# TensorE's expert loop: eight blocks a turn in place of two, and the next block's register values loaded among the products

## The reference

```python
gate_logits = x @ w_gate                                   # 2048 x 8
topk_vals, topk_idx = jax.lax.top_k(softmax(gate_logits), 2)
gu = jnp.einsum('bsd,edh->ebsh', x, w_gate_up)             # 256 -> 2 x 1024 for each expert
g, u = jnp.split(gu, 2, axis=-1)
act = silu(g) * u
expert_out = jnp.einsum('ebsf,efd->ebsd', act, w_down)     # 1024 -> 256
out = x + jnp.einsum('bse,ebsd->bsd', gate_probs, expert_out)
```

## Time and profile before

| | us |
|---|---|
| median of three runs | 480.5 |
| the three runs | 467.39, 480.5, 480.98 |
| the profiled execution, its own time | 467.51 |
| its span | 465.7 |
| TensorE busy, of the span | 438.6 (94%) |
| VectorE busy | 313.3 (67%) |
| ScalarE busy | 224.7 (48%) |
| GpSimd busy | 191.2 (41%) |

### The profile page before, as it was taken

The page is one execution under the profiler, slowest core; times in us unless marked ns, Lnnn a source line. Parts: engine busy times, 40 slices in busy tenths (PEclk is TensorE's granted clock), DMA queues, the critical chain, the costliest instruction groups (busy, mean ns, idle before and its releaser), DMA issues.

```text
span 465.7 us, 10519 instructions
## 1 busy us (share of the span) xinstructions
PE 438.6 (94%) x2336; PEld 357.0 (77%) x2337; DVE 313.3 (67%) x813; ACT 224.7 (48%) x484; POOL 191.2 (41%) x210
## 2 busy tenths in 40 slices
PE   8899788899999999999999999999999999999980
PEld 4688444688888888888888888888888888888870
DVE  2678998887587568857775467867775487745530
ACT  2577863564554345536543345636543364434330
POOL 4355203445553445433453335533453435543211
PEclk9999679899999999999999999999999999999996
DMA  8654142355155315442551114542542124211121
GB/s 222 193 177 151 49 181 68 115 159 154 30 126 150 85 23 123 125 114 68 157 125 34 23 23 113 124 125 68 157 119 41 23 73 108 34 35 24 12 24 11
DMA packets 28605, 43.87 MB, mean 94 GB/s; under 512 B 2833, under 2 KB 22219, under 8 KB 28587
## 3 DMA queue, kind: packets, MB, share of 16 engines
q1 hardware_dynamic: 20465, 32.80, 22.5%
q0 software_dynamic: 7520, 10.39, 13.3%
q10 hardware_dynamic: 602, 0.47, 0.4%
HBM read 34.02 MB, written 9.64 MB: 94 GB/s over the span
## 4 chain that ended last, share of the span: by engine, by line
PE 83%; DVE 8%; issue 3%; DMA 2%; POOL 2%; ACT 0%; SPq 0%; DVEq 0%; POOLq 0%
PE bank L1308 46%; PE bank L1328 15%; PE bank L1330 8%; PE bank L1318 7%; PE bank L1292 2%; DVE token_sel L686 2%; PE bank L1105 1%; DMA x_sb<-in_x 1%; PE bank L1149 1%; DVE x_sb L645 1%; DMA out<-y_sb,out_i 1%; DVE w L375 1%; POOL rstd L474 1%; PE bank L1135 1%; PE bank L1172 0%
## 5 line engine op out<-in xcount | busy, mean ns | idle before, releaser
L1308 PE MATMUL bank<-w,tokT_hi 128*128 (+1 forms) x624 | 175.1, 402 | 3.1 <-DVE w L375 1.1
L1047 ACT ACTIVATE gated<-bank,row_rstd 128x512 f32<-128x512 f32 x78 | 53.6, 687 | 187.7 <-PE bank L1308 187.7
L1308 PEld LDWEIGHTS bank<-w,tokT_hi 128*128 128x128 f32 x624 | 113.0, 189 | 28.8 <-issue 6.3
L1328 PE MATMUL bank<-w,aT_hi 128*128 (+1 forms) x312 | 119.5, 417 | 1.1 <-DVE y_sb L859 1.1
L838 DVE SCALAR_TENSOR_TENSOR act<-bank,row_rstd,gated 128x512 f32<-128x512 f32 x78 | 58.5, 749 | 83.6 <-ACT gated L1047 83.6
L555 POOL DMA_INDIRECT out<-y_sb,out_i x39 | 61.9, 1588 | 99.3 <-DVE y_sb L859 99.3
L1308 PE MATMUL bank<-w,tokT_lo 128*128 (+1 forms) x312 | 97.4, 394 | 0.0
L1330 PE MATMUL bank<-w,aT_lo 128*128 (+1 forms) x312 | 87.6, 281 | 0.0
L542 POOL TENSOR_TENSOR tok<-tok,beta_b 128x256 f32<-128x256 f32 x38 | 29.3, 770 | 105.4 <-DMA tok<-rows_d,gather_i 105.4
L1308 PEld LDWEIGHTS bank<-w,tokT_lo 128*128 128x128 f32 x312 | 58.8, 189 | 13.3
L1328 PEld LDWEIGHTS bank<-w,aT_hi 128*128 128x128 f32 x312 | 58.8, 188 | 11.7 <-issue 1.3
(11 more groups left out here) (168 smaller groups left out, 421.6 us busy)
## 6 DMA issues: line engine op xcount, KB each, us to landing
raw<-in_L_ffn_w_gate_up SPq DMA_DIRECT2D x32, 512.0 KB, 3.8
raw<-in_L_ffn_w_down SPq DMA_DIRECT2D x16, 512.0 KB, 3.7
rows_d<-x_sb SPq DMA_DIRECT2D x8, 264.0 KB, 2.8
x_sb<-in_x SPq DMA_DIRECT2D x8, 256.0 KB, 6.9
out<-x_sb SPq DMA_DIRECT2D x8, 256.0 KB, 3.4
out<-y_sb,out_i POOLq DMA_INDIRECT x39, 3.8
tok<-rows_d,gather_i POOLq DMA_INDIRECT x38, 3.8
cap<-in_mask_BxSxS_ik SPq DMA_DIRECT2D x1, 462.0 KB, 6.9
```

The source lines that it names most:

```text
L1047: act_e.activation(gated[:, h, :], ps_g[h][:, :], ACT.Silu, scale=row_rstd[:, s:s + 1]).then_inc(gated_set, 1)
L1308: ins = pe.matmul(ps[:, :], tokens_[:, s, k, :], w.rearrange("p a g d -> p (a g) d"), start=(k == 0 and tokens_ is tokT_hi and part == 0), ...
L1328: pe.matmul(ps_y[:, :], aT_hi[:, h, c, :], w.rearrange("p a t d -> p (a t d)"), start=(h == 0 and c == 0), stop=False, skip_group_check=True)
```

## The change

TensorE's stream alone is changed. The loop has eight blocks a turn (UNROLL = 8) and four turns, for blocks 5 to 36; blocks 1 to 4 and 37 and 38 are written out. `gate_up` takes an argument `then`: with it, the words of the block after are loaded behind the six products of k = 0 of the second half, and `experts` gets place and weights as arguments. At the first block of a turn, and at block 37, nothing has been loaded ahead; there three words are loaded at the start (the place of the block before, and place and weights of the block itself).

```diff
-            def gate_up(b, s, h, place):
+            def gate_up(b, s, h, place, then=None):
...
+                    if k == 0 and then is not None:
+                        known = (place_of(then), weights_of(then))
...
-            def experts(b, s, place_before=None, last=False):
-                place = place_of(b)
-                if later(b, 2):
-                    weights_there(b)
...
+            def experts(b, s, place, weights, place_before, known=True):
+
+                pe.wait_ge(w_lo, weights)
                 gate_up(b, s, 0, place)
-
-                if place_before is None:
-                    place_before = place_of(b - 1)
                 turn_act(b - 1, 1)
...
-                gate_up(b, s, 1, place)
+                following = gate_up(b, s, 1, place, then=b + 1 if known else None)
...
-            with pe.Fori(1, NBLK // 2 - 1) as i:
-                place = experts(2 * i + 1, 1)
-                experts(2 * i + 2, 0, place)
...
+            with pe.Fori(0, (NBLK - 7) // UNROLL) as i:
+                first = UNROLL * i + 5
+                before_, at = place_of(first - 1), place_of(first)
+                weights = weights_of(first)
+                for j in range(UNROLL):
+                    following = experts(first + j, (j + 1) % 2, at, weights, before_, known=(j + 1 < UNROLL))
+                    if j + 1 < UNROLL:
+                        before_, (at, weights) = at, following
```

More of the change, by code:

```diff
@@ L67, in build @@
     GROUPS = [range(0, 4), range(4, 8), range(8, 12), range(12, 14), range(14, 16)]
+    UNROLL = 8
+    assert (NBLK - 7) % UNROLL == 0
     ACT_PLACES = [range(0, 2), range(2, 4), range(4, 6), range(6, 8), range(8, 12), range(12, 14), range(14, 15)]
@@ L1310, in gate_up @@
                                             stop=(k == KD - 1 and tokens_ is tokT_lo))
+                    if k == 0 and then is not None:
+                        known = (place_of(then), weights_of(then))
                 ins.then_inc(gu_ps, 1)
+                return known if then is not None else None
             def turn_act(b, h):
@@ L1335, in place_of, with weights_of @@
                 return pe.value_load(place_t[0:1, bass.ds(b, 1)], min_val=0, max_val=PIECES)
-            def weights_there(b):
-                pe.wait_ge(w_lo, pe.value_load(weights_t[0:1, bass.ds(b, 1)], min_val=PIECES, max_val=PIECES * E))
-            def experts(b, s, place_before=None, last=False):
-                place = place_of(b)
-                if later(b, 2):
-                    weights_there(b)
-                else:
-                    pe.wait_ge(w_lo, pe.value_load(early_t[0:1, 0:1], min_val=GU, max_val=PIECES * E))
+            def weights_of(b):
+                return pe.value_load(weights_t[0:1, bass.ds(b, 1)], min_val=PIECES, max_val=PIECES * E)
+            def experts(b, s, place, weights, place_before, known=True):
+                pe.wait_ge(w_lo, weights)
                 gate_up(b, s, 0, place)
-                if place_before is None:
-                    place_before = place_of(b - 1)
                 turn_act(b - 1, 1)
@@ L1353, in experts @@
                 down(b - 1, 0, place_before)
-                if not last:
+                if known is not None:
                     turn_tok(b + 1, 1 - s)
-                gate_up(b, s, 1, place)
+                following = gate_up(b, s, 1, place, then=b + 1 if known else None)
                 turn_act(b, 0)
                 down(b - 1, 1, place_before)
-                return place
+                return following
             turn_tok(0, 0)
@@ L1367, in _ @@
             pe.wait_ge(tables_set, 1)
-            place = experts(1, 1, 0)
-            experts(2, 0, place)
-            with pe.Fori(1, NBLK // 2 - 1) as i:
-                place = experts(2 * i + 1, 1)
-                experts(2 * i + 2, 0, place)
-            place = experts(NBLK - 2, 1)
-            place = experts(NBLK - 1, 0, place, last=True)
+            place = [0, place_of(1)]
+            early = pe.value_load(early_t[0:1, 0:1], min_val=GU, max_val=PIECES * E)
+            place_2, weights = experts(1, 1, place[1], early, place[0])
+            place_3, weights = experts(2, 0, place_2, weights, place[1])
+            place_4, weights = experts(3, 1, place_3, weights, place_2)
+            experts(4, 0, place_4, weights, place_3, known=False)
+            with pe.Fori(0, (NBLK - 7) // UNROLL) as i:
[6 more added lines that the diff above has]
+                        before_, (at, weights) = at, following
+            before_, at = place_of(NBLK - 3), place_of(NBLK - 2)
+            place_last, weights_last = experts(NBLK - 2, 1, at, weights_of(NBLK - 2), before_)
+            experts(NBLK - 1, 0, place_last, weights_last, at, known=None)
             turn_act(NBLK - 1, 1)
-            down(NBLK - 1, 0, place)
-            down(NBLK - 1, 1, place)
+            down(NBLK - 1, 0, place_last)
+            down(NBLK - 1, 1, place_last)
 _INS = ["x", "ctx_1024", "mask_BxSxS2_ik1", "L0_xattn_gamma", "L0_xattn_beta", "L0_ffn_w_gate", "L0_ffn_w_gate_up",
```

## The result

The changed kernel takes 464.22 us in the median of 22 runs (461.37 to 478.31), the kernel before 467.19 (464.04 to 481.36, 22 runs). The profiled execution of the changed kernel has a span of 460.1 us and a time of 461.84.

What follows compares the result with a forecast made beforehand. TensorE's own stream was taken as the bound, with late starts to win back: 4.15 - 0.74 = 3.4 us less, taken from a 480.5 us median to 477.1 us; range 462.5 to 485.

Steps and rivals of the forecast that it cites:

- What bounds the kernel: Expert blocks: TensorE's own stream bounds; no other engine or transfer holds it; 4.4 us are lost in the loop.
- The low part, then branch and loads: Block starts: where VectorE's low part is late, branch and loads outlast the lead; 13 of 36 starts lose 4.7 us.
- Loads taken from the starts: At 31 of 36 starts neither branch nor load remains; 4.15 of 4.7 us go, block 13's 0.54 stays.
- Loads among the products: Second halves, before k = 1: queued products hide 1.5 us of loads; cost nothing, else 0.1 to 0.3 us a block.
- The five starts that keep their loads: Blocks 5, 13, 21, 29, 37 load three words: block 13 loses 0.74 us more, the others 0, or 0.35 each.
- The sum: Whole kernel: 4.15 - 0.74 = 3.4 us less, between 2.0 and 3.8; the profiled 467.5 becomes 464.1 us.
- the time from which the sum was taken: Whole kernel: a median of 480.5 us, as two of three runs lay 13.1 to 13.5 us above the profiled execution.
- the 0.35 case: Whole kernel: chance 0.35 that the median lies at the profiled execution's level, giving 464.1 us.
- the test for it: Instruction queue q8: about four more packets, none between the second turn's start and the loop's end; otherwise the too-long loop shows.
- The rival's price: Branches back to 13, 21, 29: if the loop no longer fits, 2.8 us each, 7.8 in all, slower; chance 0.3.
- The moved stall: At `down`: TensorE may wait for VectorE's low part instead, shrinking the gain to 0 to 1.5 us; chance 0.1.

Runs made afterwards that it cites:

- e2_loads_only: Against the kernel before: still two blocks a turn, but the even block's words load among the odd block's products, odd blocks load three; four runs, 477.0 to 488.56 us.
- e6_two_pairs: Against the changed kernel: the two words are loaded twice among the products, the first pair thrown away; 479.4 us, ratio 1.0317 to the kernel before.
- e4_even_start: Against the changed kernel: the loop begins at block 4, blocks 1 to 3 written out, four turns for 4 to 35; ratio 0.9970 to the kernel before.
- e5_no_loop: Against the changed kernel: all 38 blocks written out on TensorE, each block's words loaded among the previous block's products; 460.67 us, ratio 0.9923 to the kernel before.
- e1_branch_only: Against the kernel before: eight blocks a turn, but each block's two words still loaded at its start; ratio 0.9958 to the kernel before.

## Why the prediction was right or wrong

**What bounds the kernel: right.** TensorE's own stream bounds it, and what was to be had were the late starts. The low part, then branch and loads, is the order in which a start gets late: by it 9.5 us were expected of `e2_loads_only`, and 10.94 came. What it left out is that a start on time shortens the lead of the next.

**Loads taken from the starts: right.** 4.15 us were said to go; 12 of the 13 late starts are gone, 4.2 us. The 0.03 us at undisturbed even starts stayed (2.77 against 2.73), as taken.

**Loads among the products: right, with its cover.** Cost 0, and the cover is the queue, which `e6_two_pairs` overdrew by the expected amount (15 to 22 us, measured 18). The lead that is left did not grow, as I had said it would: 0.8 us were said for block 5 and 1.0 or more for the others, and it is 0.7 in odd blocks and 0.9 to 1.1 in even ones. With the pair between them, the addresses of k = 0 and k = 1 are 1.7 to 1.9 us apart in most blocks, not the 1.5 that I took. The second half's first address waits for VectorE's `act` too, so that time saved earlier may be spent there; that was not tested.

**The five starts that keep their loads: right.** 1.28 us were expected at block 13 (0.54 + 0.74) and 1.39 were measured; 5, 21, 29 and 37 lost nothing. `e4_even_start` shows that this was also luck of the place: with the five starts one block earlier 3.7 us are lost.

**The sum: right.** 3.4 us were forecast, 3.4 (0.74% of 465) measured in the runs below 470 us and 3.15 to 3.35 in the trace. The low end of its range about the fast run, 467.5 - 3.8, is 463.7 and not 463.5.

**The step that failed is the last one, the time from which the sum was taken.** "As two of three lie there, a median does likelier than not (0.65): 480.5 - 3.4 = 477.1 us". Two runs of three were taken for a rate. Over 22 runs of before only 9 take that long, so its median is 467.19 and not 480.5, and that of the changed kernel is 464.22, 12.9 us below the forecast. The sum belonged to the execution whose profile it was made from; I moved it by 13 us with nothing in the profile for it. What the runs show in those 13 us is a clock on its 1.2 GHz level from about 20 to 50 us, ahead of all changed code, in the two profiles of such runs (of other kernels than these two), and a mean clock that is lower in each of them. With dummy products in the first 23 us no run was long. Why the clock falls in one execution and not in the next stays open.

That 464.22 lies so near the 464.1 of the 0.35 case is luck. The execution that this case started from was among the slowest of before's shorter runs (467.5, their median is 464.96), and the median of all 22 is likewise at the upper end of the changed kernel's shorter ones (461.8). The profiled execution took 461.84, 2.3 us less than 464.1, as 2.65 us were gone ahead of block 2.

**The rivals.** The body of 4.5 packets is kept, with four more packets by the end and none between the second turn and the loop's end, as the test for it said. The rival's price was low, at 2.8 us a branch: it is 3.6, near the upper bound of 3.8, and 4.7 to 7.2 with the clock that falls behind it. It was not far off: twelve blocks a turn bring it. The moved stall did not come as described: `down` does not wait for the low part in the changed kernel's loop, and the smallest lead there is 0.5 us (0.16 in `e5_no_loop`). But a milder form is real: `e1_branch_only` gives back half of its expected gain through shorter leads. It does not show in the changed kernel, whose leads shrink too (28's from 0.99 to 0.75 us), as there is nothing left at those starts to be late.

## What to carry to other kernels

Where one engine bounds a kernel and its waits are empty, measure the distance between starts, and look at what its sequencer does behind its own waits: two register loads, 0.74 us each, cost nothing here behind 2 us and more of queued work, and up to their full time right behind a wait that ends late. Unrolling to get rid of branches is worth it only together with moving what stands at the branch, and only up to the length of code that the engine keeps; beyond it write the loop out altogether or stay below. Make a forecast of a time against the execution that the sum was read from, and take the share of long runs from many runs or not at all.

## What I had not expected of the hardware

- TensorE keeps a loop of 1,417 instructions and not one of 1,699. A taken branch to code that is gone takes 3.56 to 3.61 us, and the clock falls to 1.2 GHz behind it, 4.7 to 7.2 us in all. Straight code (5,919 instructions, `e5_no_loop`) is fetched without any loss that shows.
- The granted clock can stay on 1.2 GHz for 27 us while TensorE is busy nearly all the time (28.6 of 30 us). With seven dummy products in idle time of the first 23 us, none of 25 runs took 470 us or more.
- A taken branch within the kept code costs 207 to 243 ns on TensorE. The Trainium skill ("Advanced Engine Details and Errata", "Control Flow Timing") has about 108 for compare-and-branch; the measurement decides.
